# The same instructions of a two-block attention kernel, put in another order by new tables of numbers

## The reference, cut to what matters

```python
z = _mha(x, x, Wq1, Wk1, Wv1, mask0, causal=True)
x1 = _layernorm(x + z, ln1_g, ln1_b)
z = _mha(x1, context, Wq2, Wk2, Wv2, mask1, causal=False)
x2 = _layernorm(x1 + z, ln2_g, ln2_b)
z = jnp.maximum(x2 @ fc1_w.T + fc1_b, 0.0) * mask0
z = (z @ fc2_w.T + fc2_b) * mask0
h = _layernorm(x2 + z, ln3_g, ln3_b)
...
scores = jnp.einsum('bhqd,bhkd->bhqk', qh / np.sqrt(dk).astype(qh.dtype), kh)
scores = scores + bias + graph_attn_bias
weights = jax.nn.softmax(scores, axis=-1)
out = ctx @ wo + bo + residual
```

## Time and profile before

| | us |
|---|---|
| median of 3 runs | 377.48 |
| lowest and highest run | 376.44, 379.8 |
| time of the profiled execution | 376.83 |
| its span | 375.0 |
| PE busy, PEld busy | 348.3, 261.8 |
| DVE, ACT, POOL busy | 291.5, 241.2, 240.0 |

### The profile page before, as it was taken

One profiled execution on the slowest core, in us unless ns is written; L12 is line 12 of the kernel. 1 busy time (PEld: TensorE's weight loads), 2 busy tenths in 40 slices (PEclk: granted clock), 3 DMA queues, 4 the chain that ended last, 5 costly groups with the idle time before them and its releaser, 6 DMA issues.

```text
span 375.0 us, 13323 instructions
## 1 busy us (share of the span) xinstructions
PE 348.3 (93%) x5375; PEld 261.8 (70%) x5383; DVE 291.5 (78%) x836; ACT 241.2 (64%) x567; POOL 240.0 (64%) x376
## 2 busy tenths in 40 slices
PE   7588989999999999999999999999999897999998
PEld 3255547677878777777878787877688685777765
DVE  3456887898879988979889897889787966787551
ACT  1317556586767767586768776777768575577641
POOL 0243272848485859677686959596868667777763
PEclk9969999999999999999999999999999999999999
DMA  5992000020100022100102000023010010110000
GB/s 167 352 301 105 2 2 3 2 59 2 58 3 2 3 66 63 58 4 10 59 10 66 2 9 3 2 66 121 2 56 13 2 66 9 58 54 16 9 9 16
DMA packets 13181, 17.88 MB, mean 48 GB/s; under 512 B 1601, under 2 KB 10177, under 8 KB 13121
## 3 DMA queue, kind: packets, MB, share of 16 engines
q1 hardware_dynamic: 13120, 17.04, 14.7%
HBM read 15.99 MB, written 1.05 MB: 45 GB/s over the span
## 4 chain that ended last, share of the span: by engine, by line
PE 66%; DVE 9%; ACT 8%; POOL 7%; issue 5%; SPq 2%; DMA 1%; ACTq 0%; POOLq 0%; DVEq 0%
PE C_E L545 6%; PE C_E L600 6%; PE C_E L561 4%; PE C_E L590 4%; PE A_E L407 3%; PE B_E L407 3%; PE A_E L426 3%; PE C_E L577 3%; PE B_E L329 3%; PE A_E L440 2%; PE B_E L426 2%; PE C_E L502 2%; ACT qT L731 1%; PE B_J L369 1%; PE B_E L440 1%
## 5 line engine op out<-in xcount | busy, mean ns | idle before, releaser
L1039 POOL TENSOR_TENSOR Sc<-Sc,C_mx 128x512 f32<-128x512 f32 x28 | 29.1, 1043 | 33.0 <-DVE C_mx L947 33.0
L989 POOL TENSOR_TENSOR A_kblk<-A_qk,cst 128x1024 f32<-128x1024 f32 x16 | 30.3, 1896 | 17.4 <-DVE A_qk L833 17.4
L731 ACT ACTIVATE qT<-C_E,bq 128x128 f32<-128x128 f32 x112 | 31.7, 370 | 13.6 <-PE C_E L545 13.6
L999 POOL TENSOR_TENSOR L_rstd<-L_ve,cst 128x1 f32<-128x1 f32 x64 | 35.1, 549 | 5.0
L997 POOL TENSOR_TENSOR L_ve<-L_mv,cst 128x1 f32<-128x1 f32 x64 | 12.1, 189 | 39.4 <-DVE L_mv L898 38.9
L1010 POOL TENSOR_TENSOR L_xg<-L_xh,vec_sb 128x128 f32<-128x128 f32 x64 | 29.3, 458 | 11.9 <-DVE L_xh L907 11.7
L989 POOL TENSOR_TENSOR B_kblk<-B_qk,cst 128x1024 f32<-128x1024 f32 x16 | 30.3, 1897 | 2.6 <-DVE B_qk L833 2.4
L545 PE MATMUL C_E<-x3T,wq_sb 128*128 128x128 f32 x224 | 31.2, 283 | 0.0
L1048 POOL TENSOR_TENSOR Pc<-Pc,C_rd 128x512 f32<-128x512 f32 x28 | 28.9, 1042 | 2.1 <-DVE C_rd L957 1.8
L600 PE MATMUL C_E<-wo_sb,C_zT 128*128 128x128 f32 x224 | 27.9, 278 | 1.1 <-DVE Sc L937 1.1
L545 PEld LDWEIGHTS C_E<-x3T,wq_sb 128*128 128x128 f32 x224 | 27.1, 191 | 1.5 <-issue 0.6
(11 more groups left out here) (179 smaller groups left out, 1021.9 us busy)
## 6 DMA issues: line engine op xcount, KB each, us to landing
f<-in_fs SPq DMA_DIRECT2D x16, 512.0 KB, 3.7
out<-osb SPq DMA_DIRECT2D x16, 64.0 KB, 1.6
xTs<-in_xT SPq DMA_DIRECT2D x1, 768.0 KB, 9.2
xs<-in_x SPq DMA_DIRECT2D x1, 768.0 KB, 11.1
cs<-in_ctxn SPq DMA_DIRECT2D x1, 768.0 KB, 12.8
cTs<-in_ctxT SPq DMA_DIRECT2D x1, 768.0 KB, 9.3
vec_sb<-in_vecs SPq DMA_DIRECT2D x1, 640.0 KB, 6.7
wk_sb<-in_wk SPq DMA_DIRECT2D x1, 512.0 KB, 4.2
```

Of the source, the lines that this page charges most:

```text
L731: last = act.activation(place(n).qT[:, 4 * g + j], place(n).E[g][:, j * P:(j + 1) * P], ACT.Identity, bias=bq8[:, 4 * g + j:4 * g + j + 1] ...
L989: tt(a.kblk[:], a.qk[:, 1].unsqueeze(1).to_broadcast([P, 8, P]), at["rmask"].unsqueeze(2).to_broadcast([P, 8, P]), ALU.mult).then_inc(a.s_ ...
L999: tt(l.rstd[:], l.ve[:], at["power"], ALU.pow).then_inc(l.s_rstd, 1)
L1039: tt(v, v, place(n).mx[:, 8 * g:8 * g + 8].unsqueeze(2).to_broadcast([P, 8, S]), ALU.subtract).then_inc(C.s_sub, 1)
```

## The change

All numbers of TURN, SHIFT and MOVES are new. Nothing else differs: the steps, their instructions, their sizes, tiles and semaphores are the same, and each engine has the same set of instructions as before. Here are two lines of each table, of 26, 12 and some 420.

```diff
 TURN = """
-C.loadf=-26.883018006 C.store=-24.459548631 A.m0=-21.572682671 C.chi=-21.300857442 A.q0=-21.027749677
+K.warm=-66.407281317 C.whi=-60.010756906 C.wlo=-59.502518230 C.wvhi=-59.320930686 C.wvlo=-57.980547281
...
 SHIFT = """
-A -0.333844284 -0.02399688 0.001006103 0.005662062 0.000684014 -6.4756e-05 -0.009918065 -0.004591085 0.005988389 -0.000354003 -0.002972939 -0.000877511 -0.0027435 0.001324956 -0.008417483 -0.021297864
+A -0.014331001 -0.006547543 0 0 0 -0.00628471 0.000865751 0.002528775 0 -0.003014199 -0.004379321 0 -0.000503047 0.001449143 -0.005382541 0.005737598
...
 MOVES = """
-C.loadf#0=-6.829135146 C.loadf#1=8.964620020 C.loadf#2=8.951187109 C.loadf#3=7.995587130 C.loadf#4=7.088674585
```

More of the change, by code:

```diff
@@ L1072 @@
[L1072 to L1081, removed]
@@ L1087 @@
[L1087 to L1091, removed]
@@ L1092 @@
-C.gb=-13.923085715 C.xh=-13.912894527 L.warm=0.056971470
+K.warm=-66.407281317 C.whi=-60.010756906 C.wlo=-59.502518230 C.wvhi=-59.320930686 C.wvlo=-57.980547281
+C.obias=-57.531515186 C.bvo=-57.091479992 A.m0=-41.261991213 A.qk=-41.146114983 A.qkv=-41.091603914
+A.q0=-40.970109446 A.e0=-40.905401262 C.chi=-40.810251669 A.nz=-40.573198230 A.kblk=-40.445040191
+A.cnt=-40.441545830 A.cut=-40.407658111 A.v=-40.377985311 A.e=-40.211979638 A.max_0=-40.098686370
+A.max_1=-40.091993051 A.sub_0=-40.008018684 A.sub_1=-39.990180755 A.exp_0=-39.934589020 A.exp_1=-39.916653084
@@ new lines @@
+A.pt_0=-39.880210866 A.pts_0=-39.868748062 C.clo=-39.855405073 A.pt_1=-39.846505196 A.pts_1=-39.813014480
+A.pv_0=-39.699632247 A.pv_1=-39.692981441 A.zts=-39.669235185 C.k_0=-39.613900846 A.z=-39.612337157
+C.ks_0=-39.586198067 C.k_1=-39.583685983 C.ks_1=-39.535444295 A.y=-39.502520920 A.zn=-39.502518090
+A.rstd=-39.485222708 A.st=-39.476404937 A.xh=-39.378340759 A.gb=-39.284936931 B.cm=-38.738688619
+B.am=-38.706738740 B.tr=-38.479080761 B.xts=-38.442885468 B.qkv=-38.358414384 B.q0=-38.282488608
@@ new lines @@
+B.e0=-38.253392620 B.nz=-38.246368259 B.qk=-38.224245747 B.cnt=-38.192456138 B.cut=-38.179555339
+B.kblk=-38.148129788 B.v=-38.104143699 B.e=-37.970375234 B.max_0=-37.886247631 B.max_1=-37.853612974
+B.sub_0=-37.751265160 B.exp_0=-37.716469893 B.sub_1=-37.681075367 B.pt_0=-37.629109820 B.pts_0=-37.574979045
+B.exp_1=-37.573562734 B.pt_1=-37.504659714 B.pts_1=-37.453359111 B.pv_0=-37.386551731 B.pv_1=-37.381385824
+B.zts=-37.343032815 B.z=-37.278347657 B.zn=-37.221024752 B.y=-37.142345830 B.rstd=-37.064913069
@@ new lines @@
+C.fadd_1=-35.745918686 C.max_0=-35.710083921 C.sub_0=-35.693349916 C.exp_0=-35.593476454 C.max_1=-35.588933304
+C.sub_1=-35.559340763 C.den_0=-35.530319534 C.nrm_0=-35.402451267 C.exp_1=-35.320926988 C.den_1=-35.264542679
+C.nrm_1=-35.140841748 C.pt_0=-35.055034596 C.pts_0=-35.052854624 C.pt_1=-35.031207042 C.pts_1=-35.003962021
+C.zt=-34.956300665 C.zts_0=-34.917335546 C.zts_1=-34.902109742 C.x3c=-34.862598839 C.o=-34.645600772
+C.y=-34.569474947 C.store=-34.034585741 C.st=-34.030405163 C.rstd=-33.894092449 C.xh=-33.861533460
@@ L1115 @@
[L1115 to L1124, removed]
```

876 lines of the change are left out of this document (445 added, 431 removed).

## The result

The changed kernel takes 365.56 us (median of 4 runs, 365.48 to 366.46) beside 377.74 us (4 runs, 376.44 to 379.8): a ratio of 0.9678, with a 95% interval of 0.9632 to 0.9725. It is 3.2% faster. The forecast was 375.0 us, in a range from 371.8 to 378.4.

A forecast was written before the change was run, and what follows sets the result against it. PE, busy 348.3 of 375.0 us, was taken to bound the kernel. Start -1.1, middle 0 and end -0.8 made -1.9 on 376.83, so 374.9, stated as 375.0 us, range 371.8 to 378.4.

The forecast's parts named there:

- The start: Steps up to B.e#1: gains in the first pairs less a loss at A.e#1, -1.1 us, between -2.1 and +1.2.
- Its walk: Step-by-step tracing of the start across engines, from pair 0 to B.e#1, giving the start's gains and losses.
- The blank term: Start: six blank products instead of two ahead of A.e#1 make it 0.7 us later, pair 0's gain included.
- Pair 0: Start: the earlier first exponential on ACT brings A.z#0 at 20.8 instead of 21.25, a gain of 0.45 us.
- The middle: 60 to 290 us: no idle wait repeats, so 0 us change, between -2 and +3.
- the fourth rival: Middle: new neighbours hide more weight loads, making PE denser than its idle time allows; 372.7 us, chance 0.05.
- The end: Last 85 us, where the chains run out: moved steps shorten waits, -0.8 us, between -2 and +0.8.
- The clock's rival: Start: earlier transposes fill PE's idle 2.24 us, so the clock does not fall; 372.8 us, chance 0.22.
- The slower one: Middle: DVE becomes late, one 0.4 us wait in each of eleven pairs; 379.5 us, chance 0.10.

The follow-up runs named there:

- s_tail: Kernel before, with only the steps from A.e#15 to the end in the new order; 376.09 us, ratio 0.9945.
- s_mid: Kernel before, with only the steps between C.e#1 and A.e#15 in the new order on every engine; 373.98 us, ratio 0.9909.
- n_exp0: Changed kernel with the cast C.whi#0 put back ahead of the exponential A.exp_0#0 on ACT; 365.5 us, ratio 0.9674.
- m_DVE: Kernel before, with only DVE's queue in the new middle order and all other engines in the old; 402.15 us, ratio 1.0659.
- pe_old: PE's row of the kernel before, run alone after loads and fills without waits on other engines; period 19.49 us per pair.
- pe_new: PE's row of the changed kernel, run alone after loads and fills without waits on other engines; period 19.30 us per pair.
- light_old: Kernel before, with wide ACT, DVE and POOL operations cut to 128 of 512 columns from pair 5 (chain C: pair 2); 364.43 us, ratio 0.9658.
- m_noPE: Kernel before, with ACT, DVE, POOL and SyncE in the new middle order and PE in the old; 393.76 us, ratio 1.042.

## Why the prediction was wrong

**The start** (forecast -1.1, measured -1.69 at `B.e#1`). Its walk was good where it went from one engine to the next: `A.e#1` to `A.e#2` gave 0.80 for 0.75 and `A.e#2` to `A.e#3` 0.86 for 0.75; `A.e#3` to `B.e#1` 0.22 for 0.3, and the wait that came next was POOL's masked keys, as said. The blank term had the wrong sign. `A.e#1` came 0.19 us later where 0.7 was forecast, in an execution that began 1.13 us late; from `A.e#0` on it was 0.94 earlier. Pair 0 gave twice what I had: `A.z#0` stands 8.76 us behind `A.e#0` instead of 9.68, 0.92 earlier where 0.45 was forecast. From `A.z#0` to `A.e#1` it then takes 4.03 us instead of 4.05, where I had 1.15 more. The blank products were six, as said, but the clock was back at 23.6, before the first of them, and not at 25.2. That the clock would be the same as in the one trace of before was a premise without a reason: it differs from execution to execution of the same kernel.

**Where the walk stopped.** I took the middle to begin behind `B.e#1`. From there to `A.e#5` another 1.36 us were gained, which no term held.

**The middle** (forecast 0, between -2 and +3; measured -5.24 from `A.e#5` to `A.e#15`). This is the step that failed. The term rested on "of the 5.2 idle microseconds no wait repeats", and its lower bound on half of that idle time. Both take shown idle time for all the waiting. PE waited 0.83 us per pair and the new order took 0.36 of that away; another 0.19 came from the row itself, which I had named in the fourth rival and given a chance of 0.05, since "no row shows that a neighbour changes a product's time". The difference is only seen between starts, and I had read lengths. That rival's time, 372.7, was too small a gain even so: it priced the neighbours alone. Its sentence on the Trainium skill (Perfetto Trace Analysis, Identifying the Most-Contended Engine) was right that the busy share overstates how near PE is to its limit: PE showed 98% where 0.83 of 20.32 us was waiting. The room up to PE's own row alone was 4%, though, not the 23% that the weight loads' share gives.

**The end** (forecast -0.8, measured -2.0). `B.e#15` waited 0.39 us instead of 0.87, and 1.05 us were gained from `B.e#14` to it, not 0.3. `B.pt_1#14` waited for `B.sub_1#14` as said. From `B.e#15` to the end 0.25 were gained for 0.5, and 0.71 came before `B.e#14` (23.38 us from `A.e#15` instead of 24.09). Neither the new end alone (s_tail, 24.23) nor the new middle alone (s_mid, 24.10) has these 0.71, so they come only with both, and why is open.

**The rivals.** The clock's rival was half right in its effect (3.4 us at the half clock instead of none), but not for its reason, as n_exp0 shows. The slower one had DVE late in the middle; in the changed kernel DVE is busier (205.20 of 230 us) and PE waits less. Late steps on DVE were real in m_DVE, though, at 24 us and not 4.4. (By its own terms, 376.83 + 4.4 - 1.9, that rival's time was 379.3 and not 379.5.)

## What to carry to other kernels

A queue that shows 98% busy can still wait: read the period from the starts of one recurring step, and get the floor by running the queue's row alone, before bounding what a new order can give. An order over several in-order queues is one thing; a step moved on one queue, or a cheaper row for one engine, is worth only what the steps behind it on the others allow. One trace is one execution: look at the granted clock of all of them before a half clock is put down to an order. And a cheap filler step between a producer and its consumer may be what hides a copy.

## What the runs showed of the hardware

- A matmul step's pitch depends on its neighbour: eight of the same products take 0.86 or 0.97 us to the next start (pe_old, pe_new). Moves that took 7 and 4 entries into smaller tiles out of the rows saved 0.28 and 0.24 us for each.
- The pitch of 0.86 us repeats within about 0.01 us from pair to pair in pe_old, and the periods of s_mid and the changed kernel agree within 0.02 us.
- In the traces the half clock at the start came in three sizes only, 6.8, 3.4 or 0 us, and two kernels with the same first pairs (before and light_old) differed in it. In the traces of s_mid (from 318.0) and m_noPE (from 330.2) the clock fell a second time, for 3.4 us.
- The half clock differs between executions of one kernel: the mean granted clock of the kernel before was 0.986, 0.991, 0.995 or 1.0, and its median time 379.3, 377.8, 376.4 or 376.0 us.
- A wait of PE can be longer than the idle time shown for it (0.54 us for 0.31), and one of about 0.2 us isn't shown at all.
